# A four-layer graph network in one kernel: mask order at the gate halves, elu placement and x places in the attention layer, the last columns in two pieces

## What is computed

```python
# layer 0: a projection, then four gated aggregations (kk = 0..3)
alpha = jnp.tanh(x_i @ gw[:x.shape[1]] + x_j @ gw[x.shape[1]:] + gb)
msg = norm[:, None] * alpha * x_j
gnn_out = gnn_out + jax.ops.segment_sum(msg, col, num_segments=n_nodes)
# layer 1: x @ W.T + bias, W scattered from edge_weight
# layer 2: relu(segment_sum(h[src] * norm) + b), h = x @ W
# layer 3: attention over the edges
e = jnp.exp(-jax.nn.leaky_relu(al[src] + ar[dst], negative_slope=NEG_SLOPE))
rowsum = jax.ops.segment_sum(e, src, num_segments=N)
h_prime = jax.ops.segment_sum(e[:, None] * h[dst], src, num_segments=N)
return jax.nn.elu(h_prime / (rowsum[:, None] + EPS))
```

## Time and profile before

| what | value |
|---|---|
| runs | 992.0, 993.5, 993.78 us; median 993.5 us |
| profiled execution | 993.59 us, of which the span of the trace is 991.7 us |
| PE busy | 969.9 us, 98% of the span |
| DVE, ACT, POOL busy | 674.9 us (68%), 443.1 us (45%), 140.0 us (14%) |
| granted TensorE clock, mean | 0.997 of full speed |
| gates, 124.9 to 409.2 us | PE busy 283.03 of 284.30 us |
| attention, 875.0 to 974.6 us | PE busy 99.60 of 99.60 us |
| the end, 974.6 to 991.7 us | PE busy 11.04 of 17.10 us |

### The profile page before, as it was taken

One profiled execution on the slowest core, in us unless ns is written; L12 is line 12 of the kernel. 1 busy time (PEld: TensorE's weight loads), 2 busy tenths in 40 slices (PEclk: granted clock), 3 DMA queues, 4 the chain that ended last, 5 costly groups with the idle time before them and its releaser, 6 DMA issues.

```text
span 991.7 us, 14256 instructions
## 1 busy us (share of the span) xinstructions
PE 969.9 (98%) x5170; PEld 805.5 (81%) x5170; DVE 674.9 (68%) x1223; ACT 443.1 (45%) x662; POOL 140.0 (14%) x191
## 2 busy tenths in 40 slices
PE   5999999999999999999999999999999999999997
PEld 4788878888888888888888888888888888888885
DVE  7887798789788779468874115233346564988886
ACT  5689864544554547223335446002012322445543
POOL 3022510000000001223331000010100000333331
PEclk9999999999999999999999999999999999999999
DMA  7256490000000005543421040732231130101223
GB/s 253 90 187 227 123 272 1 1 22 0 0 21 0 0 0 117 98 147 127 138 96 65 1 171 14 282 113 101 85 128 69 69 122 1 44 22 63 85 85 123
DMA packets 25892, 88.28 MB, mean 89 GB/s; under 512 B 3370, under 2 KB 3370, under 8 KB 25696
## 3 DMA queue, kind: packets, MB, share of 16 engines
q1 hardware_dynamic: 14960, 52.82, 15.1%
q0 software_dynamic: 10880, 34.74, 11.4%
HBM read 59.23 MB, written 33.56 MB: 94 GB/s over the span
## 4 chain that ended last, share of the span: by engine, by line
PE 90%; DVE 5%; ACT 2%; DMA 1%; issue 1%; ACTq 0%; DVEq 0%
PE ps L611 21%; PE ps L2205 11%; PE ps L2179 11%; PE ps L2099 9%; PE ps L2100 9%; PE ps L2101 9%; PE ps L2155 5%; PE ps L2151 5%; PE ps L594 2%; DMA xin<-in_x 1%; PE ps L2022 1%; PE ps L2024 1%; PE ps L2023 1%; PE ps L1949 1%; PE ps L1965 1%
## 5 line engine op out<-in xcount | busy, mean ns | idle before, releaser
L2099 PE MATMUL ps<-g_hi,mask_hi 128*128 128x512 f32 x400 | 157.4, 394 | 2.1 <-DVE mask_lo L1571 2.1
L2101 PE MATMUL ps<-g_hi,mask_lo 128*128 128x512 f32 x400 | 155.8, 390 | 0.0
L2100 PE MATMUL ps<-g_lo,mask_hi 128*128 128x512 f32 x400 | 155.7, 389 | 0.0
L1114 ACT ACTIVATE mask<-ps,v 128x640 f32<-128x640 f32 x80 | 63.5, 793 | 111.3 <-PE ps L2101 52.9
L2205 PE MATMUL ps<-y_all,att_hi 128*128 128x512 f32 x400 | 110.0, 393 | 1.4 <-DVE att_lo L1820 1.4
L2099 PEld LDWEIGHTS ps<-g_hi,mask_hi 128*128 128x128 f32 x400 | 75.1, 188 | 20.5 <-DVE mask_lo L1571 3.3
L2101 PEld LDWEIGHTS ps<-g_hi,mask_lo 128*128 128x128 f32 x400 | 75.1, 188 | 16.0
L2205 PEld LDWEIGHTS ps<-y_all,att_hi 128*128 128x128 f32 x400 | 74.0, 188 | 17.3 <-DVE att_lo L1820 1.6
L2100 PEld LDWEIGHTS ps<-g_lo,mask_hi 128*128 128x128 f32 x400 | 75.1, 188 | 15.0
L611 PE MATMUL ps<-w,hT_hi 128*128 128x512 f32 x320 | 86.6, 392 | 0.0
L577 ACT ACTIVATE hT_hi<-ps 128x1024 fp32r<-128x1024 f32 x30 | 30.8, 1026 | 122.3 <-PE ps L594 122.1
(11 more groups left out here) (221 smaller groups left out, 1932.5 us busy)
## 6 DMA issues: line engine op xcount, KB each, us to landing
xin<-x_after SPq DMA_DIRECT2D x20, 512.0 KB, 3.3
xres<-x_after POOLq DMA_DIRECT2D x20, 512.0 KB, 3.6
x_after<-xres POOLq DMA_DIRECT2D x20, 512.0 KB, 2.9
w_raw<-in_L_gnn_W SPq DMA_DIRECT2D x8, 1024.0 KB, 10.8
x_after<-g POOLq DMA_DIRECT2D x20, 256.0 KB, 7.1
xres<-x_after SPq DMA_DIRECT2D x10, 512.0 KB, 3.3
xin<-in_x SPq DMA_DIRECT2D x9, 512.0 KB, 3.4
out_x<-xres SPq DMA_DIRECT2D x9, 512.0 KB, 2.6
```

The lines of the kernel that those rows point to most:

```text
L1114: nc.scalar.activation(mask[k][:, :], U_ALL, ACT.Tanh, bias=v[:, s:s + 1]).then_inc(tanh_ready, 1)
L2099: nc.tensor.matmul(SUMS[dd], mask_hi[k][:, cols], g_hi[:, s, :], start=(s == 0), stop=False)
L2100: nc.tensor.matmul(SUMS[dd], mask_hi[k][:, cols], g_lo[:, s, :], start=False, stop=False)
L2101: last = nc.tensor.matmul(SUMS[dd], mask_lo[k][:, cols], g_hi[:, s, :], start=False, stop=(s == T - 1))
```

## The change

The diff has three parts. **First, the gate halves:** at the end of a half DVE does `mask_rest` for steps 8 and 9 ahead of `mask_of` for the next half's steps 0 and 1, and ACT copies both last high parts in step 7, ahead of the next half's first `tanh`.

```diff
@@ half_act (ACT)
-                elif s < T - 1:
+                elif s < T - TANH_LEAD:
                     mask_hi_of(q, s + 1)
-                elif not last:
+                elif s == T - TANH_LEAD:
+                    mask_hi_of(q, T - 2)
+                    mask_hi_of(q, T - 1)
+                elif s == T - 1 and not last:
                     mask_hi_of(q + 1, 0)
@@ half_dve (DVE)
-                elif not last:
-                    mask_of(q + 1, 1 - h, s + 2 - T)
                 if not (isinstance(q, int) and q == 0):
                     mask_rest(q, s)
                 elif 0 < s < T - 1:
                     mask_rest(q, s + 1)
+                if s >= T - 2 and not last:
+                    mask_of(q + 1, 1 - h, s + 2 - T)
```

```diff
@@ SP
         sp.wait_ge(al_ready, T)
-        load3(0, 0)
-        load3(0, 1)
-        with sp.Fori(0, HT - 1) as i:
+        for i in range(2):
+            for b in range(2):
+                load3(i, b)
+        for i in range(HT - 1):
             for b in range(2):
                 store3(i, b)
-                load3(i + 1, b)
+                if i + 2 < HT:
+                    load3(i + 2, b)
@@ attention_dve (DVE)
-                if not first and s in (7, 8):
+                if not first and not last and s in (7, 8):
                     elu_end(GRP * (grp - 1) + s - 7, grp - 1, s - 7)
+            if last:
+                for j in range(GRP):
+                    elu_end(GRP * (grp - 1) + j, grp - 1, j)
...
-        with dve.Fori(1, GROUPS - 1) as grp:
+        for grp in range(1, GROUPS - 1):
@@ ACT
+        act.wait_ge(gat_added, T - GRP - 1)
         gat_take(T - 2, 0)
         elu_act(T - 2, 0)
+        act.wait_ge(gat_added, T - GRP)
```

```diff
@@ PE
-        for s in range(T):
-            last = gat_step(s, 1, [1])
-        last.then_inc(gat_ready, 1)
+        for q in range(2):
+            for s in range(T):
+                last = quarter_step(s, q)
+            last.then_inc(gat_ready, 1)
@@ quarter_step (new, PE)
+            cols = slice(P, 2 * P)
+            of = slice(HID + q * QUARTER, HID + (q + 1) * QUARTER)
+            for left, rights in ((att_hi[s][:, cols], (y_hi[s], y_lo[s])), (att_lo[s][:, cols], (y_hi[s],))):
+                for right in rights:
+                    last = nc.tensor.matmul(LAST_QUARTERS[q], left, right[:, of], start=(s == 0 and len(rights) == 2 and right is y_hi[s]),
+                                            stop=(s == T - 1 and len(rights) == 1))
@@ SP
+        pieces = (slice(0, HID), slice(HID, HID + QUARTER), slice(HID + QUARTER, D))
+        for n, cols in enumerate(pieces):
+            sp.wait_ge(gat_added, T + n)
+            sp.dma_start(out[(T - 1) * P:N, cols], res3[(HT - 1) % 2][1][0:N - (T - 1) * P, cols]).then_inc(gat_stored[1], 16)
```

More of the change, by code:

```diff
@@ L56 @@
 BANK = 512
+QUARTER = 256
 GRP = 2
@@ L175, in build_program @@
     e_sum = at("e_sum", [P, GC], F32, R_X + 6 * KIB)
+    res3 = [[xres[0], xres[1]], [at(f"res3_{j}", [P, D], F32, R_W + (48 + 4 * j) * KIB) for j in range(GRP)]]
     gat_sums = [at(f"gat_sums{j}", [P, D], F32, R_W + (32 + 4 * j) * KIB) for j in range(GRP)]
@@ L447, in build_program @@
     gat_exp_ready = sem("gat_exp_ready")
-    gat_landed = sems("gat_landed", 2)
+    gat_landed = [sems(f"gat_landed{parity}_", 2) for parity in range(2)]
     gat_added = sem("gat_added")
@@ L476, in build_program @@
     AGG = [ps[:, 4 * j * BANK:(4 * j + 2) * BANK] for j in range(GRP)]
+    LAST_QUARTERS = [ps[:, n * BANK:n * BANK + QUARTER] for n in (5, 6)]
     DEN = [ps[:, (2 + j) * BANK:(2 + j) * BANK + 2] for j in range(GRP)]
@@ L791, in load3 @@
         def load3(i, b):
-            sp.dma_start(xres[b][:, :], x3_dram[rows(2 * i + b), :]).then_inc(gat_landed[b], 16)
+            sp.dma_start(res3[i % 2][b][:, :], x3_dram[rows(2 * i + b), :]).then_inc(gat_landed[i % 2][b], 16)
         def store3(i, b):
-            settled(sp, gat_added, 2 * i + b + 1)
-            sp.dma_start(out[rows(2 * i + b), :], xres[b][:, :]).then_inc(gat_stored[b], 16)
-            settled(sp, gat_stored[b], 16 * (i + 1))
+            sp.wait_ge(gat_added, 2 * i + b + 1)
+            sp.dma_start(out[rows(2 * i + b), :], res3[i % 2][b][:, :]).then_inc(gat_stored[b], 16)
+            sp.wait_ge(gat_stored[b], 16 * (i + 1))
         sp.wait_ge(al_ready, T)
-        load3(0, 0)
-        load3(0, 1)
-        with sp.Fori(0, HT - 1) as i:
+        for i in range(2):
+            for b in range(2):
+                load3(i, b)
+        for i in range(HT - 1):
             for b in range(2):
                 store3(i, b)
-                load3(i + 1, b)
+                if i + 2 < HT:
+                    load3(i + 2, b)
         store3(HT - 1, 0)
[L807 to L811, removed]
+        pieces = (slice(0, HID), slice(HID, HID + QUARTER), slice(HID + QUARTER, D))
+        for n, cols in enumerate(pieces):
+            sp.wait_ge(gat_added, T + n)
+            sp.dma_start(out[(T - 1) * P:N, cols], res3[(HT - 1) % 2][1][0:N - (T - 1) * P, cols]).then_inc(gat_stored[1], 16)
+        sp.wait_ge(gat_stored[1], 16 * (HT - 1 + len(pieces)))
     @block.gpsimd
@@ L917, in load2 @@
         def load2(i, b):
-            pool.dma_start(xres[b][:, :], x2_dram[rows(2 * i + b), :]).then_inc(agg_landed[b], 16)
+            pool.dma_start(xres[b][:, :], x2_dram[rows(2 * i + b), :]).then_inc(res_landed[b], 16)
         def store2(i, b):
@@ L1328, in _ @@
         attention_act(GROUPS - 1, range(T), False, True)
+        act.wait_ge(gat_added, T - GRP - 1)
         gat_take(T - 2, 0)
         elu_act(T - 2, 0)
+        act.wait_ge(gat_added, T - GRP)
         gat_take(T - 1, 1, slice(0, HID))
         elu_act(T - 1, 1, slice(0, HID))
[L1333 to L1336, removed]
+        for q in range(2):
+            end = slice(HID + q * QUARTER, HID + (q + 1) * QUARTER)
+            act.wait_ge(gat_ready, T + 1 + q)
+            nc.scalar.activation(elu_neg[1][:, end], LAST_QUARTERS[q], ACT.Exp, scale=rden[:, 1, 1:2]).then_inc(gat_exp_ready, 1)
+            nc.scalar.activation(gat_sums[1][:, end], LAST_QUARTERS[q], ACT.Relu, scale=rden[:, 1, 1:2]).then_inc(gat_pos_ready, 1)
     @block.vector
@@ L1844, in elu_end @@
             dve.wait_ge(gat_pos_ready, m + 1)
[L1845 removed]
+            nc.vector.tensor_tensor(res[:, cols], elu_neg[j][:, cols], gat_sums[j][:, cols], ALU.add).then_inc(gat_added, 1)
         def attention_dve(grp, steps, first, last):
@@ L1887, in _ @@
         end = slice(HID, D)
-        nc.vector.tensor_scalar(xres[1][:, end], xres[1][:, end], 1.0, None, ALU.subtract).then_inc(elu_added, 1)
+        res = res3[(GROUPS - 1) % 2][1]
+        nc.vector.tensor_scalar(res[:, end], res[:, end], 1.0, None, ALU.subtract).then_inc(elu_added, 1)
         dve.wait_ge(elu_added, T + 1)
[L1890 to L1894, removed]
+        for q in range(2):
+            end = slice(HID + q * QUARTER, HID + (q + 1) * QUARTER)
+            dve.wait_ge(gat_exp_ready, T + 1 + q)
+            nc.vector.scalar_tensor_tensor(elu_neg[1][:, end], elu_neg[1][:, end], 1.0, res[:, end], ALU.min, ALU.add).then_inc(gat_chain, 1)
+            dve.wait_ge(gat_chain, GAT_STEPS * T + 1 + q)
+            dve.wait_ge(gat_pos_ready, T + 1 + q)
+            nc.vector.tensor_tensor(res[:, end], elu_neg[1][:, end], gat_sums[1][:, end], ALU.add).then_inc(gat_added, 1)
     @block.tensor
@@ L2208, in gat_step, with quarter_step @@
             return last
+        def quarter_step(s, q):
+            cols = slice(P, 2 * P)
[4 more added lines that the diff above has]
+                                            stop=(s == T - 1 and len(rights) == 1))
+            return last
         def row_sums(j):
```

8 lines of the change are left out of this document (4 added, 4 removed).

## The result

The changed kernel takes 988.76 us (median of 5 runs, 987.48 to 989.06) against 993.5; the ratio is 0.995 with a 95% interval of 0.994 to 0.9961, so it is faster by about 4 to 6 us. A later comparison beside the kernel before, on one chip, gave 987.93 against 993.18, ratio 0.9946 (0.9932 to 0.996).

A forecast was written before the change was run, and what follows sets the result against it. TensorE (PE), busy 98% of the span, was taken to bound the kernel. Terms of -0.9 (gates), -1.43 (attention), +0.4 and -0.94 (last columns) made -2.9 us on 993.59: forecast 990.6 us, range 989.0 to 992.4.

The forecast's parts named there:

- What is late next: Even gate halves: DVE's chain hands back most of the stall's gain, leaving 0.3 us per pair, -0.9 us for three.
- some 0.2 us: Even gate halves: how far DVE's chain can follow, its 0.24 us wait less 0.06 to 0.1 that ACT adds.
- Rival (b): Gate halves: no gain, as later mask and split on ACT delay DVE's chain equally; 991.5 us, chance 16%.
- rival (a): Gate halves: the whole gate gain arrives, 2.1 us instead of 0.9; 989.4 us, chance 10%.
- The attention stall: Last attention group, step 9: PE's wait goes once both elu_end stand behind the last att_lo; -1.43 us, weak bound -1.2.
- my cover: Last group: both elu_end end by 977.0, 0.35 us ahead of DVE's next wide operation, due at 977.35.
- Rival (e): Last group: the moved elu_end chain delays tile 8 and the tail, giving back about 1 us; 991.6 us, chance 11%.
- Own places and loops: Own places for x and written-out loops of DVE and SP: 0 us, with +0.3 as the bound.
- The last columns: Last 512 columns as two 256-column pieces: +0.4 us on PE, -0.94 us in the tail behind, net -0.5.
- (c): Last columns: each short product waits a little for its own load, +2.6 us on top; 993.2 us, chance 5%.
- (d): Last columns: loads run one behind the other, +4.5 us instead of +0.4; 994.7 us, chance 7%.
- signs of being wrong: Half 2's step 6 not held by DVE, 256-column step above 0.14 us, or ACT's last piece starting while DVE does the earlier.

The follow-up runs named there:

- late_split: The changed kernel with g_rest of tiles 7, 8, 9 in steps 6, 7, 8 of the even halves instead of 3, 4, 5; median 988.54 us beside 987.93.
- gate_dve_order: The kernel before with only DVE's half of the gate order, ACT unchanged; 990.55 us in one profiled execution.
- elu_in_steps: The changed kernel with elu_end of tiles 6 and 7 back in steps 7 and 8 of the last group; 989.39 us in one profiled execution.

## Why the prediction was right or wrong, point by point

**The gate stall's price.** 0.7 us each, 2.1 for three, by starts and not by the 0.40 in brackets: right; `late_split` recovers 2.2.

**What is late next.** The mechanism, DVE's chain in the even halves, was right, and is shown by `late_split`. Its size was wrong: -0.9 in the sum, -1.33 measured. The step that failed is "some 0.2 us" for how far DVE's chain can follow. Two things were missed. The first is DVE's slack, which I read from the bracket, 0.24 us. The row ahead of the sums in the kernel before says more:

```profile
192.92 0.81 DVE L1571 TENSOR_TENSOR mask_lo<-mask,mask_hi 128x640 fp32r<-128x640 f32 x1
```

Where DVE doesn't wait, the sums start 0.73 us behind this one's start (192.55 to 193.28 in the changed kernel), so they could have started at 193.65 and not at 193.98: the slack by starts is 0.33 us. DVE's chain does come 0.07 later than before (`mask_lo` at 68.04 us behind the first mask matmul instead of 67.97), inside the 0.06 to 0.1 that I allowed, and the sums start 0.26 us earlier against the first mask (193.28 - 124.51 = 68.77, before 193.98 - 124.95 = 69.03). `gate_dve_order` has that delay too with ACT unchanged, so it doesn't come from ACT's new order. The second thing: the five sums. They took 3.39 us (193.98 to 197.37) when they waited for PE and take 3.30 now (193.28 to 196.58): 0.09 more. That PE paced them is my reading; no run tests it. With the 0.1 for the late load that makes 0.45 for each pair, three times 0.44 measured. The waits of the loads stand in steps 5 and 6, not from step 3 on as I had written among the signs. Rival (b) fell, and rival (a) was true only of a kernel that also relieves DVE.

**The attention stall.** 1.43 forecast, 1.46 measured, and by `elu_in_steps` for the reason given. Both `elu_end` took 4.88 us (969.78 to 974.66) where I had allowed 5.64, since the second starts 2.40 us behind the first there, and not 2.82. They were over 0.94 us ahead of DVE's next wide operation at 975.60, not the 0.35 of my cover; that operation starts 1.57 us behind the first row sums (975.60 - 974.03), before 1.51 (978.79 - 977.28). Rival (e) fell.

**Own places and loops.** Put at 0, with +0.3 as the only bound. The places are worth nothing by themselves, but leaving them out costs 1.9 us in L, which I had not priced. DVE's loop gives some 0.35 us outside the span; my sum held the 1.9 around the span fixed, and its bound here had no gain in it. That was a step without a reason.

**The last columns.** 0.120 us a step forecast, 0.121 measured. PE loses 0.48 (983.61 - 976.32 = 7.29 from row sums to last start, before 986.39 - 979.58 = 6.81), forecast 0.4; behind it DVE's end comes 0.93 sooner, forecast 0.94. Rivals (c) and (d) fell with it. The store was the error: I left 2.68 as it is, with -0.3 as bound, and it fell to 2.19. One of my signs of being wrong did appear: ACT's first operation on the last piece starts at 983.92, when DVE is still at the first piece (983.83 to 984.25). I had let the first piece's operations run during PE's 3.6 us, but on DVE they stand behind the leftover of the first columns, which ends at 983.34. It cost nothing, with 0.17 us of idle time left ahead of the last piece.

**The sum.** The stretches show -4.2 us where I had -2.9, and three terms failed, all on the same side: the gates (-1.33 for -0.9, 0.4 us), the time of the last store (-0.5 for 0), and the written-out loops (-0.4 outside the span for 0). The first two had bounds, -2.1 and -0.3; the third had none below zero. These 1.3 us alone would have given 989.3, inside the range. The other 0.5 us to 988.76 would fit the level that I counted from: 993.5, the median of three runs, when all 72 runs of the kernel before on record have a median of 992.9. That this is the reason isn't shown, since the kernel before had 993.5 in the same comparison, and five later runs of the changed kernel gave 987.93.

## What to carry to other kernels

A stall that is taken away is worth its full price only if the engine that caused it can follow: here 0.44 us of 0.7, with 0.33 us of slack by starts next on that engine. Look for the place, even a whole phase later, where a consumer starts right behind its producer without a wait in brackets, and move work from there too. Measure a change of a few tenths of a per cent by distances between marks in the trace, since those repeat within 0.1 us where whole runs differ by 2. Work moved behind the last deadline needs its buffers checked: here the two shared places for x cost 1.9 us where the move gives 1.46.

## What the runs showed of the hardware

The time from DVE's end to the end of the span depends on the bytes of the last store, 98 rows from 98 partitions: 2.64 to 2.71 us with 2 KB a row, 2.15 to 2.19 with 1 KB. Products of 256 columns with a weight load each run at 0.121 us, those of 226 at 0.112 and of 512 at 0.230, half the columns cost about half the time. A load's own row lasts 0.19 us at each of these widths, more than 0.121 and 0.112, so loads that follow one another overlap. The start of the program up to the first mask matmul takes from 123.2 to 125.2 us in 14 profiles, and makes nearly all of the difference between two profiles of one kernel (1.26 of 1.26 us for the changed kernel, 0.52 of 0.52 for the kernel before); what moves in it wasn't followed up. A hardware loop on DVE went with 0.3 to 0.4 us more outside the span, for which the trace has no row.

Some DVE and POOL operations take longer where they stand beside each other. In the kernel before, tile 6 in the last group:

```profile
969.02 1.79 POOL L949 TENSOR_TENSOR e_part<-e_part,att_e 128x256 f32<-128x256 f32 x1 [1.23 <-DVE att_e L1815]
...
970.25 1.64 DVE L1845 TENSOR_TENSOR xres<-elu_neg,gat_sums 128x1024 f32<-128x1024 f32 x1
```

This DVE operation takes 1.64 or 1.65 us in all eight places where POOL's operation runs into it, and 1.23 where POOL has nothing to do (973.43 in the changed kernel, 982.01 in the kernel before). POOL's own takes 1.63 to 1.80 us in those places, mostly 0.74 elsewhere. Behind the last `att_lo`, where POOL is done, each `elu_end` so takes 0.42 us less of DVE's time. No run was made to test the cause.
